# Where the last rounds read layer 1 out of PSUM, and the precision of four late units, in a three-layer interaction network

## The chip, the core and the metric

One core of a Trainium2 chip runs the whole program. The metric is the device time of one execution in microseconds, lower is better. The core has a matrix engine (TensorE, PE in the rows; its weight loads are PEld), a vector engine (VectorE, DVE), a scalar engine (ScalarE, ACT), a general engine (GpSimd, POOL) and a queue that issues transfers (SyncE, SP). Each engine executes its own instructions in the order in which they are written and meets the others by semaphores.

## The reference

1024 rows of 39 looked-up fields, each a vector of 16 numbers, pass through three layers of pairwise products. Layer i multiplies each field of the input with each field of the layer's state and contracts the products with a weight matrix of 128 columns; half of the outputs of the first two layers becomes the next state, the rest goes straight to the sum. Three dense layers follow.

```python
for i, (W, b) in enumerate(zip(Ws, bs)):
    Wr = W.reshape(F0, Fk, L)
    z = jnp.einsum('bfd,bgd->bfgd', x, h)
    cur = jax.nn.relu(jnp.einsum('bfgd,fgl->bld', z, Wr) + b[None, :, None])
    if i != n - 1:
        h = cur[:, :L // 2]
        direct = cur[:, L // 2:]
    else:
        direct = cur
    outs.append(direct)
...
h = jnp.maximum(h @ W_top1 + b_top1, 0.0)
h = jnp.maximum(h @ W_top2 + b_top2, 0.0)
y = h @ W_top3
```

## The kernel before

The 1024 x 16 columns are cut into 32 steps of 512 columns. A software pipeline runs over rounds r = -3 to 31. In round r, units 0 to 9 contract layer 1 of step r + 1, units 10 to 19 layer 2 of step r, and units 20 to 23 layer 0 of step r + 3. The last rounds are shorter: rounds 29 and 30 have units 0 to 19 alone, and round 31 has units 10 to 19. (r, u) below is unit u of round r. A unit is up to 256 rows of products by 512 columns, and its kind says how it is made:

- F, full precision: VectorE makes the product in SBUF (L618), TensorE contracts it with two full matrix products, which the trace shows as four instructions (L987). ScalarE and GpSimd have no part in it.
- G: VectorE makes the product, ScalarE copies it rounded to `zh` (`hi`, L816), GpSimd subtracts to get the rest `zl` (L359), and TensorE makes six faster instructions: two each of `zh` with the weights' low part (L1004), `zh` with the high part (L1005), and `zl` with the high part (L1012).
- P: the same split with the product held in PSUM (`curY`), in two halves of 512 columns; VectorE makes product and rest of each half (L684, L696), ScalarE rounds each (L801). In round 29 the parts of a P unit follow it at a distance of two and four units, in round 30 at one and two: the first rest and the second product stand before the product of the unit behind it, the second rest before that of the unit two behind.
- D: like G, with the rest made by VectorE (L705).

Rounds 29 and 30 both have the kinds `GPGGFGPGGF FGPGGFGPGG` for units 0 to 19. Units 3, 8, 14 and 19 are F in the early rounds; from round 25 or 26 on `kind` makes them G, with weights of their own (`wh_late`, `wl_late`).

The rings: products lie in a ring of 7 slots, `zh` and `zl` in rings of 4. The semaphore `z_ready` counts products made, `z_used` counts units that TensorE has finished.

When a layer's sum is complete, ScalarE reads it out of PSUM with bias and relu. `take0` and `take1` do this for layers 0 and 1 in seven instructions each (all L850): number 6, called `DIRECT`, writes the part that goes to the sum, numbers 0 to 5 write copies of the next state to the PSUM tile `h1` or `h2`. `take1(r, i)` reads layer 1 of step r + 1. `take2(s)` reads layer 2 of step s in one instruction, at unit 1 of round s + 1 (`LAST_AT`), after a wait until TensorE has finished unit (s, 19). Which unit each read of layer 1 follows on ScalarE is written out in `round_` of ScalarE: up to round 28, `DIRECT` after unit 18, 0 to 3 after unit 20, 4 and 5 after unit 21; in rounds 29 and 30 all seven in a row at the round's end.

Who waits for the reads of `take1(29, ...)`: VectorE's `sum_direct(30)`, a short reduction (L709) which stands behind the product of (30, 3), and VectorE and TensorE before unit (30, 10). Who waits for `take1(30, ...)`: `sum_direct(31)`, and TensorE before the dense layers (L1104, L1110, L1118, L1126), which stand between rounds 30 and 31. After round 31 a short end of the dense layers for the last 128 rows follows (L1156 to L1174).

Of the kernel before, what the change touches and what calls it, by code (L numbers as in the profile page):

```python
# [14 lines left out]
B, F, D, L = 1024, 39, 16, 128  # L15
# [5 lines left out]
STEPS = B * D // N  # L21
# [15 lines left out]
UNITS = len(KINDS)  # L37
A_END, C_END = 10, 20
# [6 lines left out]

LATE_A, LATE_C = (3, 8), (14, 19)
LATE = LATE_C + LATE_A
LATE_FROM = 25

POOL_FROM = 11  # L50
# [2 lines left out]
def present(r, u):  # L53
    if u < A_END:
        return -1 <= r <= STEPS - 2
    if u < C_END:
        return 0 <= r <= STEPS - 1
    return -3 <= r <= STEPS - 4


def kind(r, u):
    if ((r >= LATE_FROM and u in LATE_C) or (r > LATE_FROM and u in LATE_A)):
        return "G"

    k = KINDS[u]
    if k == "P":
        return "P" if r in IN_PSUM else "D"
    return "D" if k == "G" and (r < 0 or (r == 0 and u < POOL_FROM)) else k


def fresh(r):

    return (r + 3) % PER_B == 0
# [72 lines left out]
def cin_tower(nc, dense, ids, tables, w_top1, b_top1, w_top2, b_top2, w_top3, w0, w1, w2, b0, b1, b2, out):  # L146
# [4 lines left out]
    with ExitStack() as ctx:  # L151
        def sb(name, shape, dt=F32):
            return ctx.enter_context(nc.sbuf_tensor(name, shape, dt))
# [36 lines left out]
        wl = sb("wl", [P, UNITS - nf, 2, L], F32R)  # L190
        wh_late = sb("wh_late", [P, len(LATE), 2, L], F32R)
        wl_late = sb("wl_late", [P, len(LATE), 2, L], F32R)

        def full_at(u):
            return KINDS[:u].count("F")
# [116 lines left out]
        def bank(r, layer):  # L312

            if r < 0:
                return curY if layer == 0 and r != -2 else curM[r == -2]

            return xk[:, :] if (r, layer) == (STEPS - 3, 2) else curM[(r + (layer - 1) % 3) % 2]
# [25 lines left out]
        def _(pool):  # L343
# [9 lines left out]
            def subtract(r, u):  # L353
                n = split_rows(u)
                before = ring_before(r, u, NL)
                if before is not None:
                    pool.wait_ge(z_used, NUM[before] + 1)
                pool.wait_ge(hi_ready, SNUM[r, u] + 1)
                nc.gpsimd.tensor_tensor(zl[0:n, SNUM[r, u] % NL, :], z[0:n, z_slot(r, u), :],  # L359
                                        zh[0:n, SNUM[r, u] % NH, :], ALU.subtract).then_inc(lo_pool, 1)  # L360

            def weight_lo_late(n):
                pool.wait_ge(w_hi, HI_OPS + n + 1)
                nc.gpsimd.tensor_tensor(wl_late[:, n, :, :], wf[:, full_at(LATE[n]), :, :], wh_late[:, n, :, :],
                                        ALU.subtract).then_inc(w_lo, 1)

            def round_(r):
# [16 lines left out]
                for n, u in enumerate(spread):  # L384
                    if kind(r, u) == "G":
                        subtract(r, u)
                    if r == LATE_FROM and 2 <= u < 2 + len(LATE):
                        weight_lo_late(u - 2)
# [388 lines left out]
        def _(act):  # L777
# [26 lines left out]
            def hi(r, u):  # L804
                second = behind(r, u, 1)
                if second:
                    hi_half(*second, 1)
                if kind(r, u) == "P":
                    hi_half(r, u, 0)
                elif kind(r, u) != "F":  # L810
                    n = split_rows(u)
                    act.wait_ge(z_ready, NUM[r, u] + 1)
                    before = ring_before(r, u, NH)
                    if before is not None:
                        act.wait_ge(z_used, NUM[before] + 1)
                    nc.scalar.activation(zh[0:n, SNUM[r, u] % NH, :], z[0:n, z_slot(r, u), :],  # L816
                                         ACT.Copy).then_inc(hi_ready, 1)
# [11 lines left out]
            def copy_emb(b):  # L829
                act.wait_ge(gathered[b % 2], 16 * F * (b // 2 + 1) - 16 * FIRST_FIELDS * (b % 2 == 0))  # L830
                nc.scalar.activation(emb[b % 2][:, F * D:].rearrange("p (k c) -> p k c", k=K - 1),
                                     emb[b % 2][:, 0:F * D].unsqueeze(1).to_broadcast([P, K - 1, F * D]),
                                     ACT.Copy).then_inc(emb_copied, 1)
# [8 lines left out]
            def copy_xc(t):  # L842
                act.wait_ge(turned, t + 1)
                if t >= 3:
                    act.wait_ge(xT_written[t % 2], 32 * (t // 2))
                nc.scalar.activation(xc[t % 2][:, :].rearrange("p (b d) -> p b d", d=DQ),
                                     xk_bank(t)[0:F, :].rearrange("p (d b) -> p b d", d=DQ), ACT.Copy).then_inc(xc_copied, 1)
# [4 lines left out]
            DIRECT = 6  # L852
            DIRECT_FIRST = (DIRECT, 0, 1, 2, 3, 4, 5)

            def take(i, h, cur, bias, done, to):

                if i < 2:
                    relu(h[i * H:(i + 1) * H, 0:N], cur[0:H, :], bias[0:H, :], done)
                elif i < 6:
                    p, f = (i - 2) * Q, (i - 1) % 2 * Q  # L860
                    relu(h[p:p + Q, N:2 * N], cur[f:f + Q, :], bias[f:f + Q, :], done)
                else:
                    relu(to, cur[H:P, :], bias[H:P, :], done)

            def take0(r, i):
                s = r + 2
                if i == DIRECT:
                    act.wait_ge(z_used, NUM[r - 1, UNITS - 1] + 1)
                    if s >= 2:
                        act.wait_ge(sumA, s - 1)  # L870
                if i == 0 and r >= -1:
                    act.wait_ge(z_ready, NUM[r, A_END - 1] + 1)
                take(i, h1, l0_bank(s), bias0, read0, direct[s % 2][0:H, :])

            def take1(r, i):
                s = r + 1
                if i == DIRECT:
                    act.wait_ge(z_used, NUM[r, A_END - 1] + 1)
                    if s >= 2:
                        act.wait_ge(sumA, s - 1)  # L880
                if i == 0:
                    act.wait_ge(z_ready, NUM[r, C_END - 1 if r >= 0 else UNITS - 1] + 1)
                take(i, h2, bank(r, 1), bias1, read1, direct[s % 2][H:P, :])

            def weight_hi_late(n):
                nc.scalar.activation(wh_late[:, n, :, :], wf[:, full_at(LATE[n]), :, :], ACT.Copy).then_inc(w_hi, 1)

            def take2(s):
                act.wait_ge(z_used, NUM[s, C_END - 1] + 1)
                if s >= 1:  # L890
                    act.wait_ge(sumB, s)
                relu(last[:, :], bank(s, 2), bias2[:, :], read2)

            def round_(r):
                for u in range(UNITS):
                    if present(r, u):
                        hi(r, u)
                    if r == -2 and u == UNITS - 1:
                        for i in DIRECT_FIRST:
                            take0(r, i)  # L900
                    if r == LATE_FROM and 2 <= u < 2 + len(LATE):
                        weight_hi_late(u - 2)
                    if u == SPREAD_AT and r >= 1 and fresh(r) and r <= STEPS - 4:
                        copy_emb((r + 3) // PER_B)
                    if u == LAST_AT and r >= 1:
                        take2(r - 1)
                    if u == COPY_AT and 0 <= r <= STEPS - 4:
                        copy_xc(r + 3)
                    if u == A_END - 1 and r == -1:
                        for i in DIRECT_FIRST:  # L910
                            take0(r, i)

                    if 0 <= r <= STEPS - 3:
                        for i in {8: [DIRECT], A_END: [0, 1, 2], A_END + 1: [3, 4], A_END + 2: [5]}.get(u, []):
                            take0(r, i)
                    if 0 <= r <= STEPS - 4:
                        for i in {C_END - 2: [DIRECT], C_END: [0, 1, 2, 3], C_END + 1: [4, 5]}.get(u, []):
                            take1(r, i)
                    if u == UNITS - 1 and (r == -1 or STEPS - 4 < r <= STEPS - 2):
                        for i in DIRECT_FIRST:  # L920
                            take1(r, i)

# [5 lines left out]
            for r in range(FIRST, 1):  # L928
                round_(r)
            for r in range(1, LAST):  # L930
                round_(r)
# [39 lines left out]
        def _(pe):  # L971
# [8 lines left out]
            def contract(r, u, cur, start, stop):  # L980
# [9 lines left out]
                else:  # L990
                    h, l, w = SNUM[r, u] % NH, SNUM[r, u] % NL, split_at(u)
                    w_low, w_high = wl, wh
                    if KINDS[u] == "F":
                        w, w_low, w_high = LATE.index(u), wl_late, wh_late
                        if r <= LATE_FROM + 1:
                            pe.wait_ge(w_hi, HI_OPS + w + 1)
# [204 lines left out]
```

## Time and profile before

| | us |
|---|---|
| runs | 1285.22, 1287.26, 1286.15 (median 1286.15) |
| the profiled execution's own time | 1286.31 |
| its span in the trace | 1284.2 |
| busy: PE / DVE / POOL / ACT | 1215.5 / 1113.8 / 1036.5 / 816.4 |

The span runs from the first to the last instruction; 2.1 us of the profiled execution lie around it. Busy time of PE counts overlapping instructions once. A start in the timeline is us from the span's start, followed by the duration; a figure in square brackets is the idle time of the engine before the instruction, and behind the arrow stands what ended it.

### The profile page before, as it was taken

The page shows a single profiled execution, that of the slowest core. Times are in us where ns is not written, and L with a number is a line of the kernel's source. Part 1 is how long each engine was busy: PE and PEld are TensorE (multiplying, and loading weights), DVE is VectorE, ACT ScalarE, POOL GpSimd, SP SyncE. Part 2 cuts the span into 40 slices and gives each one's busy share as a digit, 9 for nine tenths or more (in the row PEclk, how much of TensorE's full clock was granted, in tenths as well). Part 3 has the DMA queues.
Part 4 walks back from the last instruction along what each step waited for, and adds up shares of the span by engine and source line. Part 5 has one row for each costly group of instructions (what it writes and reads, how often), then busy time and mean ns, then how long its engine had stood idle before and what let it go on. Part 6 is the DMA issues. An engine that isn't in the chain of part 4 may idle for free.

```text
span 1284.2 us, 14380 instructions
## 1 busy us (share of the span) xinstructions
PE 1215.5 (95%) x4180; PEld 767.5 (60%) x4180; DVE 1113.8 (87%) x1274; ACT 816.4 (64%) x1115; POOL 1036.5 (81%) x629
## 2 busy tenths in 40 slices
PE   0598999999999999999999999999999999999899
PEld 0254566666666666666666666666666666766545
DVE  2189999999999999999999999999999999999753
ACT  1147566666676667666676667666666778777553
POOL 7458888888988888888988888888988778888733
PEclk9999999999999999999999999999999999999999
DMA  8193466655555566655555666655455665654100
GB/s 185 24 230 93 108 143 147 146 134 116 111 125 119 132 146 147 146 130 115 112 123 122 135 146 147 147 123 118 113 117 123 139 144 144 142 119 118 33 1 1
DMA packets 102510, 156.17 MB, mean 122 GB/s; under 512 B 20811, under 2 KB 32988, under 8 KB 102322
## 3 DMA queue, kind: packets, MB, share of 16 engines
q1 hardware_dynamic: 92256, 152.56, 50.2%
q0 software_dynamic: 10176, 2.70, 2.1%
q8 instruction: 33, 0.54, 0.2%
q14 instruction: 45, 0.37, 0.1%
HBM read 151.31 MB, written 6.19 MB: 123 GB/s over the span
## 4 chain that ended last, share of the span: by engine, by line
PE 80%; DVE 7%; issue 4%; POOL 4%; ACT 4%; DMA 0%; another core or an unknown queue 0%; DVEq 0%; ACTq 0%; POOLq 0%
PE curM L987 36%; PE curM L1004 13%; PE curM L1012 13%; PE curM L1005 13%; DVE z L618 4%; POOL emb L348 3%; ACT h L850 2%; PE xk L976 2%; DVE zl L705 1%; ACT zh L816 1%; DVE zl L696 1%; POOL zl L359 1%; DVE curY L684 1%; DVE z L669 0%; PE h L1110 0%
## 5 line engine op out<-in xcount | busy, mean ns | idle before, releaser
L359 POOL TENSOR_TENSOR zl<-z,zh 128x1024 fp32r<-128x1024 f32 (+1 forms) x301 | 718.4, 2396 | 146.9 <-ACT zh L816 131.0
L618 DVE TENSOR_TENSOR z<-xr,h 128x1024 f32<-128x1024 f32 x456 | 548.4, 1212 | 3.8 <-issue 3.1
L987 PE MATMUL curM<-z,wf 128*128 128x512 f32 (+3 forms) x1220 | 537.4, 600 | 1.0 <-ACT h L850 0.9
L816 ACT ACTIVATE zh<-z 128x1024 fp32r<-128x1024 f32 (+1 forms) x320 | 337.8, 1056 | 291.1 <-DVE z L618 150.6
L348 POOL DMA_INDIRECT emb<-in_tbl_dram,idx x312 | 311.5, 998 | 89.7 <-issue 54.5
L1004 PE MATMUL curM<-zh,wl 128*128 128x512 f32 (+1 forms) x816 | 374.9, 459 | 4.8 <-issue 3.2
L987 PEld LDWEIGHTS curM<-z,wf 128*128 128x128 f32 (+3 forms) x1220 | 214.7, 188 | 237.6 <-issue 217.2
L1005 PE MATMUL curM<-zh,wh 128*128 128x512 f32 (+1 forms) x816 | 321.4, 394 | 0.0
L1012 PE MATMUL curM<-zl,wh 128*128 128x512 f32 (+1 forms) x816 | 255.5, 394 | 9.6 <-POOL zl L359 5.1
L850 ACT ACTIVATE h<-curM,bias 64x512 f32<-64x512 f32 x372 | 240.4, 646 | 20.0 <-DVE z L618 9.9
L696 DVE TENSOR_TENSOR zl<-curY,zh 128x512 fp32r<-128x512 f32 x240 | 164.9, 687 | 71.0 <-ACT zh L801 69.1
L1004 PEld LDWEIGHTS curM<-zh,wl 128*128 128x128 f32 (+1 forms) x816 | 154.7, 190 | 63.9 <-issue 35.4
L1005 PEld LDWEIGHTS curM<-zh,wh 128*128 128x128 f32 (+1 forms) x816 | 154.3, 189 | 57.5 <-issue 29.9
L1012 PEld LDWEIGHTS curM<-zl,wh 128*128 128x128 f32 (+1 forms) x816 | 153.0, 189 | 49.7 <-POOL zl L359 7.5
L801 ACT ACTIVATE zh<-curY 128x512 fp32r<-128x512 f32 x240 | 141.6, 590 | 45.6 <-PE curM L1012 33.0
L684 DVE TENSOR_TENSOR curY<-xr,h 128x512 f32<-128x512 f32 x240 | 166.0, 692 | 4.1
L669 DVE TENSOR_TENSOR z<-xk,xs 117x1024 f32<-117x1024 f32 x116 | 120.6, 1080 | 1.2 <-PE curM L987 1.2
L618 DVE TENSOR_TENSOR z<-xq,h 128x1024 f32<-128x1024 f32 x64 | 77.4, 1211 | 0.0
L850 ACT ACTIVATE direct<-curM,bias 64x512 f32<-64x512 f32 x62 | 42.4, 684 | 1.6
L850 ACT ACTIVATE last<-curM,bias 128x512 f32<-128x512 f32 x31 | 21.2, 684 | 31.2 <-PE curM L987 21.0
L976 PEld LDWEIGHTS xk<-ident,emb 128*117 128x117 f32 x120 | 28.5, 285 | 13.7 <-issue 11.1
L705 DVE TENSOR_TENSOR zl<-z,zh 128x1024 fp32r<-128x1024 f32 (+1 forms) x19 | 28.6, 1507 | 5.6 <-ACT zh L816 3.8
(140 smaller groups left out, 391.0 us busy)
## 6 DMA issues: line engine op xcount, KB each, us to landing
xr<-xT SPq DMA_DIRECT2D x384, 192.0 KB
xs<-xT SPq DMA_DIRECT2D x279, 156.0 KB
xq<-xT SPq DMA_DIRECT2D x64, 256.0 KB
emb<-in_tbl_dram,idx POOLq DMA_INDIRECT x312
xs<-xT SPq DMA_DIRECT2D x62, 78.0 KB
xT<-xc SPq DMA_DIRECT2D x31, 78.0 KB
xr<-in_L_rec_W_dram SPq DMA_DIRECT2D x16, 144.0 KB
xT<-xc SPq DMA_DIRECT2D x31, 40.0 KB
```

The costliest lines, as they stand in the source:

```text
L348: nc.gpsimd.indirect_dma_start(out=emb[slot][:, f * D:(f + 1) * D], out_offset=None, in_=tables[f], in_offset=bass.IndirectOffsetOnAxis(ap ...
L359: nc.gpsimd.tensor_tensor(zl[0:n, SNUM[r, u] % NL, :], z[0:n, z_slot(r, u), :], zh[0:n, SNUM[r, u] % NH, :], ALU.subtract).then_inc(lo_poo ...
L618: return nc.vector.tensor_tensor(z[:, slot, :].rearrange("p (a n) -> p a n", a=2), x, h, ALU.mult)
L684: nc.vector.tensor_tensor(curY[:, :], xr[s % 2][:, q * N:(q + 1) * N], h[:, a * N:(a + 1) * N], ALU.mult).then_inc(done, 1)
L696: nc.vector.tensor_tensor(zl[:, SNUM[r, u] % NL, cols], curY[:, :], zh[:, SNUM[r, u] % NH, cols], ALU.subtract).then_inc(lo_dve if a == 1 ...
L801: nc.scalar.activation(zh[:, SNUM[r, u] % NH, a * N:(a + 1) * N], curY[:, :], ACT.Copy).then_inc(hi_ready if a == 0 else hi_second, 1)
L816: nc.scalar.activation(zh[0:n, SNUM[r, u] % NH, :], z[0:n, z_slot(r, u), :], ACT.Copy).then_inc(hi_ready, 1)
L850: nc.scalar.activation(dst, src, ACT.Relu, bias=bias).then_inc(done, 1)
L987: mm = nc.tensor.matmul(cur[:, :], wf[rows, full_at(u), a, :], z[rows, z_slot(r, u), a * N:(a + 1) * N], start=start and i == 0, stop=stop ...
L1004: nc.tensor.matmul(cur[:, :], w_low[rows, w, a, :], zh[rows, h, cols], start=start and a == 0, stop=False)
L1005: nc.tensor.matmul(cur[:, :], w_high[rows, w, a, :], zh[rows, h, cols], start=False, stop=False)
L1012: mm = nc.tensor.matmul(cur[:, :], w_high[rows, w, a, :], zl[rows, l, a * N:(a + 1) * N], start=False, stop=stop and a == n - 1)
```

## The change

In rounds 29 and 30, units 8 and 19 are F again, as in the early rounds: four units in all. In round 29 the read `DIRECT` of layer 1 stands after unit 18, and the six others are moved behind units 0, 1 and 2 of round 30, two at each (for unit 1, behind `take2(29)`, which stands there too). The reads of round 30 stay in a row at its end. The round numbers in the code: `STEPS` is 32, `C_END` 20, `UNITS` 24.

```diff
+SHORT, LONGER = (STEPS - 3, STEPS - 2), (8, 19)
...
 def kind(r, u):
+    if r in SHORT and u in LONGER:
+        return "F"
     if ((r >= LATE_FROM and u in LATE_C) or (r > LATE_FROM and u in LATE_A)):
         return "G"
...
                     if 0 <= r <= STEPS - 4:
                         for i in {C_END - 2: [DIRECT], C_END: [0, 1, 2, 3], C_END + 1: [4, 5]}.get(u, []):
                             take1(r, i)
-                    if u == UNITS - 1 and (r == -1 or STEPS - 4 < r <= STEPS - 2):
+                    if r == STEPS - 3 and u == C_END - 2:
+                        take1(r, DIRECT)
+                    if r == STEPS - 2 and u < 3:
+                        for i in range(2 * u, 2 * u + 2):
+                            take1(r - 1, i)
+                    if u == UNITS - 1 and r in (-1, STEPS - 2):
                         for i in DIRECT_FIRST:
                             take1(r, i)
```

## Rows read from the trace of the kernel before

**Rows 1.** Busy time by stretch: PE, PEld, DVE, ACT, POOL, then granted clock.

```profile
1165.00:1194.40 29.40, 29.34 (x115) 20.64 (x113) 25.06 (x29) 21.76 (x30) 24.68 (x11) 1.00 0.36 99
...
1203.00:1233.50 30.50, 26.28 (x96) 16.58 (x94) 21.25 (x25) 17.43 (x23) 23.20 (x10) 1.00 0.00 1
1233.50:1261.00 27.50, 27.46 (x83) 12.87 (x84) 14.00 (x14) 11.70 (x18) 6.57 (x3) 1.00 0.00 1
```

**Rows 2.** Timeline of ScalarE from (29, 17) to `take2(29)`.

```profile
1187.74 0.60 ACT L801 ACTIVATE zh<-curY 128x512 fp32r<-128x512 f32 x1 [0.31 <-DVE curY L684]
...
1190.66 4.00 ACT L850 ACTIVATE h<-curM,bias 64x512 f32<-64x512 f32 x6
1194.69 1.06 ACT L816 ACTIVATE zh<-z 128x1024 fp32r<-128x1024 f32 x1
1195.65 0.58 ACT L801 ACTIVATE zh<-curY 128x512 fp32r<-128x512 f32 x1
1196.13 0.68 ACT L850 ACTIVATE last<-xk,bias 128x512 f32<-128x512 f32 x1
```

**Rows 3.** Timeline of VectorE from products (29, 19), (30, 0) to `sum_direct(30)`.

```profile
1187.61 2.35 DVE L618 TENSOR_TENSOR z<-xr,h 128x1024 f32<-128x1024 f32 x2
...
1190.59 0.70 DVE L684 TENSOR_TENSOR curY<-xr,h 128x512 f32<-128x512 f32 x1
1196.33 0.69 DVE L696 TENSOR_TENSOR zl<-curY,zh 128x512 fp32r<-128x512 f32 x1 [5.04 <-ACT zh L801]
...
1200.52 0.68 DVE L709 TENSOR_REDUCE zq<-direct 128x128 f32<-128x512 f32 x1
```

**Rows 4.** Timeline of TensorE: (29, 19), first and sixth instruction of (30, 0).

```profile
1192.80 0.39 PE L1004 MATMUL xk<-zh,wl_late 128*128 128x512 f32 x1
...
1193.72 0.62 PE L1012 MATMUL xk<-zl,wh_late 128*128 128x512 f32 x2
1195.89 0.47 PE L1004 MATMUL curM<-zh,wl 128*128 128x512 f32 x1 [1.55 <-ACT zh L816]
...
1198.32 1.22 PE L1012 MATMUL curM<-zl,wh 128*128 128x512 f32 x2 [1.26 <-POOL zl L359]
```

**Rows 5.** Chain that ended last: unit (29, 15), of kind F, on TensorE.

```profile
1187.13 1.73 PE xk L987 x4
```

**Rows 6.** Timeline of GpSimd: last three rests of round 29, two of 30.

```profile
1185.84 7.12 POOL L359 TENSOR_TENSOR zl<-z,zh 128x1024 fp32r<-128x1024 f32 x3 [0.18 <-PE xk L1012]
...
1227.07 4.75 POOL L359 TENSOR_TENSOR zl<-z,zh 128x1024 fp32r<-128x1024 f32 x2 [1.70 <-ACT zh L816]
```

**Rows 7.** Timeline of ScalarE: round 31's `take2`, waiting on TensorE.

```profile
1275.81 0.69 ACT L850 ACTIVATE last<-curM,bias 128x512 f32<-128x512 f32 x1 [6.10 <-PE curM L1012]
```

**Rows 8.** Timeline of TensorE: what that `take2` waited for.

```profile
1275.15 0.63 PE L1012 MATMUL curM<-zl,wh_late 128*128 128x512 f32 x2
```

**Rows 9.** Timeline of ScalarE at the end of round 30.

```profile
1225.87 1.06 ACT L816 ACTIVATE zh<-z 128x1024 fp32r<-128x1024 f32 x1 [0.53 <-DVE z L618]
1227.60 1.06 ACT L816 ACTIVATE zh<-z 128x1024 fp32r<-128x1024 f32 x1 [0.67 <-DVE z L618]
1228.69 0.68 ACT L850 ACTIVATE direct<-curM,bias 64x512 f32<-64x512 f32 x1
1229.39 4.00 ACT L850 ACTIVATE h<-curM,bias 64x512 f32<-64x512 f32 x6
```

**Rows 10.** Timeline of VectorE there: product (30, 19), `sum_direct(31)`.

```profile
1226.35 1.21 DVE L618 TENSOR_TENSOR z<-xr,h 128x1024 f32<-128x1024 f32 x1
1233.50 0.69 DVE L709 TENSOR_REDUCE zq<-direct 128x128 f32<-128x512 f32 x1 [5.94 <-ACT h L850]
```

**Rows 11.** Timeline of TensorE there: ends of (30, 18), (30, 19), first dense product.

```profile
1229.53 0.73 PE L1012 MATMUL curM<-zl,wh 128*128 128x512 f32 x2 [0.31 <-POOL zl L359]
...
1231.87 0.74 PE L1012 MATMUL curM<-zl,wh_late 128*128 128x512 f32 x2 [0.69 <-POOL zl L359]
1233.54 0.70 PE L1104 MATMUL h<-dT,xs 16*128 16x512 f32 x2 [0.93 <-ACT h L850]
```

**Rows 12.** Busy time by stretch, as rows 1: the round's start, in steps of 2 us.

```profile
1198.00:1200.00 2.00, 1.69 (x4) 1.40 (x5) 2.00 (x3) 1.44 (x2) 0.26 (x1) 0.53 0.00 0
1200.00:1202.00 2.00, 2.00 (x7) 1.52 (x7) 2.00 (x3) 1.06 (x1) 1.89 (x1) 0.62 0.00 0
```

## The prediction

> **What bounds the kernel now.** I read the busy time by stretch first, then the timelines of the engines where one stretch meets the next. Round 29 belongs to TensorE: it works 29.34 of 29.40 us, without a gap [rows 1]. VectorE is ahead there: product (29, 19) is ready at 1188.82 (1187.61 and 1.21 of the two products' 2.35 us) [rows 3], and TensorE ends that unit at 1193.72 + 0.62 = 1194.34 [rows 4]. Then the lead is lost. ScalarE does the seven reads in a row, the last six from 1190.66 for 4.00 us, and only behind them the rounding of (30, 0) at 1194.69 and of the first half of (30, 1) at 1195.65 [rows 2]. TensorE stands for 1.55 us and 1.26 us [rows 4], VectorE for 5.04 us [rows 3]. From there to 1227.6 VectorE sets the pace, and TensorE has 30.50 - 26.28 = 4.22 us of idle time [rows 1]. At the round's end seven reads stand again behind the last rounding, and the dense layers start at 1233.54, when they are done [rows 9, 11]. After that TensorE works 27.46 of 27.50 us [rows 1]: what starts it earlier ends the kernel earlier, one for one.
>
> **Part 1, the four units as F.** An F unit holds TensorE 1.73 us [rows 5]. In a G unit four instructions take 1193.72 - 1192.80 = 0.92 us, 0.23 each, so six take 1.38 [rows 4]. Each unit costs TensorE 0.35 us more. It takes from ScalarE one rounding of 1.06 us [rows 9] and from GpSimd one rest of 7.12 / 3 = 2.37 us [rows 6]. In round 29 TensorE has no gap to hide it, so two units move its end from 1194.34 to 1195.04. By itself that is no loss, since (30, 0) starts at 1195.89 [rows 4]. In round 30 it disappears in the idle 4.22 us. The slot of an F product is freed by TensorE and no longer by GpSimd; the seven products until its next use take at least 7 x 1.14 = 8.0 us of VectorE (2.35 - 1.21 = 1.14 from one to the next), and TensorE's lag was 1194.34 - 1188.82 = 5.5 us, now 6.2, so no wait: cost nothing, cover 1.8 us. No transfer is added or moved.
>
> **Part 2, the reads of round 29.** `DIRECT` after unit 18 moves the rounding of the second half of (29, 17) from 1187.74 [rows 2] to some 1188.15; its rest is made behind the product (30, 0), which ends at 1189.96 [rows 3]. Cost nothing, cover 1.2 us. The rounding of (29, 19) is gone, so that of (30, 0) runs when its product is there, 1190.0 to 1191.05. Reads 0 and 1 follow (2 x 0.67, from 4.00 / 6), then the first half of (30, 1), 1192.4 to 1193.0. The 5.04 us wait of VectorE shrinks by 3.3 us.
>
> But next on ScalarE stands `take2(29)`, and it waits for TensorE to end round 29, at 1195.04. In the kernel before it ran at 1196.13, when that had long happened. A read of the same kind starts 0.03 us after TensorE's end (1275.15 + 0.63 against 1275.81) [rows 7, 8]. So ScalarE stands for 2.0 us, and behind it are queued reads 2 and 3, the second half of (30, 1), the rounding of (30, 2), reads 4 and 5. From 1195.07: 0.70 for `take2` (the spacing 1228.69 to 1229.39 [rows 9]), 2 x 0.67, 0.48 to 0.60 for the half [rows 2], 1.08 for the rounding, 2 x 0.67. The sum is 4.94 to 5.06, the end 1200.01 to 1200.13. VectorE's `sum_direct(30)` needs all seven reads; a reduction starts 0.11 us after its last read (1229.39 + 4.00 against 1233.50) [rows 9, 10]: 1200.12 to 1200.24, where it ran at 1200.52 [rows 3]. VectorE reaches this point earlier: its rest of (30, 1) can start at some 1197.8 and the product (30, 3) ends at 1199.6. The old wait of 5.04 us becomes two, for the half and for the reads, and VectorE gains 0.28 to 0.40 us; I take **0.35**. All products of the round stand behind, so they come this much earlier. TensorE and GpSimd, fed by them, are not late: (30, 0) is ready for TensorE when it comes at 1195.04.
>
> **Part 3, the end of round 30.** The rounding of (30, 19), 1227.60, is gone. `DIRECT` follows that of (30, 18): 1225.87 + 1.09 = 1226.96. Read 0 needs product (30, 19), ready at 1226.35 + 1.21 = 1227.56 [rows 10], and ScalarE is there at 1227.66. Six reads end at 1231.66, and TensorE follows 0.15 later (1233.39 against 1233.54 [rows 9, 11]), at 1231.81 in place of 1233.54: 1.73. TensorE itself: the rest of (30, 18) by GpSimd ends at 1229.45 (half of 4.75 [rows 6]) and lets it go at 1229.53; it ends at 1230.26 at the latest [rows 11], and F takes it to 1231.99: 1.55 by this bound. The wait of 0.69 us for the rest of (30, 19) is gone as well. I take **1.6**; what is late next is TensorE's F unit and the reads at once, within 0.2 us.
>
> **Sum.** 0.35 + 1.6 = 1.95 us off 1286.31 of the profiled execution, 1284.36. The median of the runs is 0.16 lower, which gives 1284.2.
>
> **The clock.** After the gaps of 1.55 and 1.26 us the granted clock falls to 0.53 and 0.62 for 4 us, the 1.2 GHz level for most of it [rows 12]. It costs nothing now, as TensorE then waits for others anyway. The Trainium skill (TensorE: Matmul & The Clock Gate, "HAM oscillation") says that a TensorE left idle is gated to half its clock until it has been busy again. It speaks against this change in one respect: TensorE comes to (30, 0) sooner, and then waits in pieces for a later supply. By that page such a gap could put the F unit at the end at half clock; the rival for it below has its price from the rows.
>
> **Rivals.** *B, the longer round 29 costs nothing.* If TensorE took the two F units without ending later, `take2(29)` would end its wait 0.70 us sooner, VectorE would gain 1.05 in place of 0.35, and the time would be 1283.5. Against it stands the missing gap, 0.06 us in 29.40 [rows 1]. For it: ends of matrix products are modelled, and the lag could be smaller than it looks.
>
> *C, the first gain is not there and the second is cut.* If the chain behind `take2(29)` runs 0.4 us longer than my sum, the 0.35 is gone; if the F unit at the end meets a falling clock, its 1.73 us doubles. Then the 1.6 becomes -0.1: 1284.55 for the first alone, 1286.3 for both. The point from which it decides is `take2(29)` ending its wait after 1195.5.
>
> *D, slower: the clock falls on the path.* The dense layers are 27.5 us of TensorE with nothing to hide a slower clock [rows 1]. Stretches of 4 us at half clock, as the one seen [rows 12], cost 2 us each there: one takes the gain back, and 10 us at the lower level would cost 5 and give 1289.2. It decides from 4 us on, and from 9 us the kernel is slower by more than 0.2%. Against it: TensorE is busy before them with F at 1230 to 1232, where it had idled 0.93 us at full clock [rows 11].
>
> *E, the reads are no longer in anyone's way.* All that the reads cost in front would come back: 3.3 us at the first, 1.6 at the second, 1281.3. It needs `take2(29)` not to wait, which needs TensorE 2 us earlier at the end of round 29. No row allows it.
>
> **How the numbers follow.** My case (A) 0.58, with its own range 1283.5 to 1285.0; B 0.17, C 0.17, D 0.06, E 0.02. Its own runs spread over 2 us, so the range for 8 in 10 is 1282.6 to 1286.3: it holds A, B and C. What a measurement of this kernel can tell from no change is about 0.2%, 2.6 us; A is 1.95, so it counts as no difference unless it is undersized by a third, B (2.65) is just over. Faster 0.27 (B, E and the edge of A), same 0.67, slower 0.06.
>
> **What would show it.** After: `take2(29)` preceded by an idle 2 us of ScalarE, ended by TensorE at about 1195.05; two waits of VectorE between 1194 and 1200.2 in place of the 5.04; `sum_direct(30)` ended by a read, near 1200.2; products from there 0.35 us earlier; no L816 after 1226.6 in round 30; first L1104 at 1231.6 to 1231.7, with at most 0.2 us idle before it. I am wrong if `take2(29)` doesn't wait, if the granted clock falls between 1225 and 1260, or if `sum_direct(30)` is more than 0.5 us off.

## The result: 0.3% faster, and two steps of the forecast found again

The changed kernel takes 1282.85 us (median, 1282.15 to 1283.9), the kernel before on the same chip 1286.49. The ratio is 0.9969, 95% interval 0.9958 to 0.998: a gain of some 4.0 us by the ratio and 3.6 by the medians. The forecast was 1284.2, no difference most likely, from a gain of 1.95 us. The profiled execution took 1283.14 us, its span 1281.4: some 1.8 us lie around the span, where 2.1 did in the kernel before.

To see where the time went I followed one kind of instruction, VectorE's short reductions, which stand at fixed places of each round. This is the kernel before (start, duration; the one in round 29 and the last one, in round 31):

```profile
1177.68 0.68 DVE L709 TENSOR_REDUCE zq<-last 128x128 f32<-128x512 f32 x1
...
1276.53 0.69 DVE L709 TENSOR_REDUCE zq<-last 128x128 f32<-128x512 f32 x1 [7.29 <-ACT last L850]
```

and this the kernel after, in rounds 29 and 30, between the rounds 30 and 31, and in round 31:

```profile
1177.01 0.68 DVE L713 TENSOR_REDUCE zq<-last 128x128 f32<-128x512 f32 x1
...
1199.31 0.69 DVE L713 TENSOR_REDUCE zq<-direct 128x128 f32<-128x512 f32 x1 [0.47 <-ACT h L854]
...
1230.57 0.69 DVE L713 TENSOR_REDUCE zq<-direct 128x128 f32<-128x512 f32 x1 [4.21 <-ACT h L854]
...
1273.67 0.69 DVE L713 TENSOR_REDUCE zq<-last 128x128 f32<-128x512 f32 x1 [7.28 <-ACT last L854]
```

They come 0.67, 1.21, 2.93 and 2.86 us earlier than in the kernel before (the middle ones against [rows 3, 10]). The first 0.67 is there from the first reduction on, at 109.00 before and 108.34 after, and stays within 0.06 up to round 29: it arises in the set-up, which the change doesn't touch. The changed rounds bring 1.21 - 0.67 = 0.54 at their start (**front** below), and 2.86 - 1.21 = 1.65 at their end (**end**), 2.19 us together. With the set-up's 0.67 and the 0.3 us that lie no longer around the span, this is the 3.17 us between the two profiled executions (1286.31 and 1283.14).

The front, on ScalarE of the kernel after: the reads of layer 1 are L854, `take2(29)` the one from `xk`.

```profile
1190.40 1.33 ACT L854 ACTIVATE h<-curM,bias 64x512 f32<-64x512 f32 x2
1191.66 0.58 ACT L805 ACTIVATE zh<-curY 128x512 fp32r<-128x512 f32 x1
1194.39 0.69 ACT L854 ACTIVATE last<-xk,bias 128x512 f32<-128x512 f32 x1 [2.15 <-PE xk L996]
1195.10 1.31 ACT L854 ACTIVATE h<-curM,bias 32x512 f32<-32x512 f32 x2
1196.35 0.57 ACT L805 ACTIVATE zh<-curY 128x512 fp32r<-128x512 f32 x1
1196.83 1.04 ACT L820 ACTIVATE zh<-z 128x1024 fp32r<-128x1024 f32 x1
1197.89 1.32 ACT L854 ACTIVATE h<-curM,bias 32x512 f32<-32x512 f32 x2
```

ScalarE stands for 2.15 us before `take2(29)`, until TensorE has ended round 29, and everything else is queued behind it. VectorE's wait of 5.04 us [rows 3] has become three, of 1.74, 2.14 and 0.47 us, the third one that of the reduction at 1199.31. These are the first two:

```profile
1192.34 0.69 DVE L700 TENSOR_TENSOR zl<-curY,zh 128x512 fp32r<-128x512 f32 x1 [1.74 <-ACT zh L805]
...
1197.03 0.69 DVE L700 TENSOR_TENSOR zl<-curY,zh 128x512 fp32r<-128x512 f32 x1 [2.14 <-ACT zh L805]
```

The end, on TensorE: the rest of (30, 18), unit (30, 19) in full precision, the first dense product with no idle time before it, where 0.93 us stood [rows 11].

```profile
1228.33 0.72 PE L1021 MATMUL curM<-zl,wh 128*128 128x512 f32 x2 [0.34 <-POOL zl L363]
1228.89 1.88 PE L996 MATMUL curM<-z,wf 128*128 128x512 f32 x4
1230.70 0.70 PE L1113 MATMUL h<-dT,xs 16*128 16x512 f32 x2
```

By stretch (columns as in rows 1), TensorE has no gap in round 29 and none in the dense layers:

```profile
1165.00:1193.50 28.50, 28.50 (x108) 19.57 (x107) 25.49 (x31) 18.74 (x25) 21.61 (x10) 1.00 0.37 100
...
1203.00:1231.00 28.00, 25.48 (x90) 15.29 (x93) 20.61 (x24) 14.72 (x21) 16.60 (x7) 1.00 0.00 1
1231.00:1258.50 27.50, 27.50 (x83) 12.69 (x77) 13.93 (x14) 11.92 (x18) 6.93 (x3) 1.00 0.00 1
```

### The profile page after: what moved, and what is told of

It reads as the page before. It is cut to its first block, busy times and chain, and to the rows that moved or that the text cites. A ratio compares the mean times of both kernels' runs of the same rounds, so it can differ in the third digit from the quotient of the medians.

```text
span 1281.4 us, 14348 instructions
## 1 busy us (share of the span) xinstructions
PE 1217.5 (95%) x4172; PEld 766.3 (60%) x4172; DVE 1113.7 (87%) x1274; ACT 811.8 (63%) x1111; POOL 1026.7 (80%) x625
## 4 chain that ended last, share of the span: by engine, by line
PE 84%; DVE 6%; issue 4%; POOL 3%; ACT 3%; DMA 0%; DVEq 0%; ACTq 0%; POOLq 0%
PE curM L996 37%; PE curM L1013 13%; PE curM L1021 13%; PE curM L1014 13%; DVE z L622 3%; POOL emb L352 3%; PE xk L985 2%; ACT h L854 1%; DVE zl L709 1%; ACT zh L820 1%; PE h L1071 1%; DVE zl L700 1%; DVE z L673 1%; PE h L1119 0%; PE h L1127 0%
## 5 line engine op out<-in xcount | busy, mean ns | idle before, releaser
L363 POOL TENSOR_TENSOR zl<-z,zh 128x1024 fp32r<-128x1024 f32 (+1 forms) x297 | 708.8, 2396 | 154.4 <-ACT zh L820 137.6
L820 ACT ACTIVATE zh<-z 128x1024 fp32r<-128x1024 f32 (+1 forms) x316 | 333.5, 1056 | 291.7 <-DVE z L622 155.2
L854 ACT ACTIVATE h<-curM,bias 64x512 f32<-64x512 f32 x372 | 240.4, 646 | 20.7 <-DVE z L622 10.8
L854 ACT ACTIVATE direct<-curM,bias 64x512 f32<-64x512 f32 x62 | 42.4, 683 | 1.6
L854 ACT ACTIVATE last<-curM,bias 128x512 f32<-128x512 f32 x31 | 21.2, 684 | 31.6 <-PE curM L996 25.5
```

The source lines that it names most:

```text
L854: nc.scalar.activation(dst, src, ACT.Relu, bias=bias).then_inc(done, 1)
```

## The experiments

For each kernel the table has the distances between its trace and the first one of the kernel before, read from the same reductions: set-up (up to round 29), front, end, and front and end together; negative is earlier. Then the difference of the medians and the ratio with its interval, against the kernel before on the same chip.

| kernel | set-up | front | end | both | medians | ratio (95%) |
|---|---|---|---|---|---|---|
| changed | -0.67 | -0.54 | -1.65 | -2.19 | -3.64 | 0.9969 (0.9958 to 0.998) |
| changed, again | -5.42 | -0.53 | -1.66 | -2.19 | -2.37 | 0.9977 (0.9967 to 0.9987) |
| units only | -6.29 | -1.59 | -1.63 | -3.22 | -3.37 | 0.9969 (0.9957 to 0.9981) |
| reads only | -6.15 | -1.20 | +1.71 | +0.51 | -0.86 | 0.9993 (0.9984 to 1.0002) |
| take2 late | -5.87 | -2.42 | -1.62 | -4.04 | -4.56 | 0.9961 (0.9947 to 0.9974) |
| before, again | -0.73 | 0.00 | +1.70 | +1.70 | +0.63 | 1.0001 (0.9992 to 1.001) |
| reads early | -1.25 | -3.21 | -1.62 | -4.83 | -6.44 | 0.9951 (0.9937 to 0.9964) |
| unit 19 only | +0.53 | -0.86 | -1.63 | -2.49 | -3.41 | 0.997 (0.9958 to 0.9982) |
| last unit only | -0.49 | 0.00 | -1.62 | -1.62 | -2.52 | 0.9979 (0.997 to 0.9988) |
| gap | +0.31 | -0.54 | -0.55 | -1.09 | -2.63 | 0.9977 (0.9967 to 0.9987) |

The four from "changed, again" to "take2 late" ran together on another chip, where the kernel before takes 1280.68 us; their set-up of -5 to -6 most likely goes with that chip, of which there is no trace of the kernel before.

The intervals reach 1.2 to 1.7 us to either side, so the times alone don't put these kernels in order among themselves. What follows on single steps rests on the traces, where front and end repeat within some 0.01 us.

**The changed kernel again.** No edit.

> The changed kernel once more, beside the others. Its timeline against the one before shows three steps: products 0.65 us earlier from the set-up on to the end of round 29, 1.21 earlier from the L713 reduction of round 30 on, 2.93 earlier from the dense layers on. Theory A (the set-up's 0.65 us and what lies outside the span are chance, other in each execution): the step of round 30 is 0.5 us and that of the end 1.7 us again, together 2.2 to 2.3 us, while the set-up's part changes in size or sign; the time is 2.3 us below the kernel before, within 0.7 us. Theory B (the changed program is also faster where nothing was changed, by its layout): the set-up's 0.65 us comes again, and the time is 3.5 to 4 us below.

Front and end repeat within 0.01 us. The distance of the set-up does not say anything across two chips; the time, 2.4 us lower by the medians and 2.9 by the ratio (1.7 to 4.2 by its interval), lies nearer to theory A and doesn't exclude B.

**Units only.**

```diff
+SHORT, LONGER = (STEPS - 3, STEPS - 2), (8, 19)
...
 def kind(r, u):
+    if r in SHORT and u in LONGER:
+        return "F"
```

> Only the four units as F; the reads of round 29 stay in a row at its end. Theory A (it is ScalarE's freed rounding of (29, 19), 1.06 us, and the place of take2(29), that count): the seven reads start 1.6 us earlier than before, since the first of them no longer waits for product (29, 19) to be rounded; the rest of the first half of (30, 1) comes at 1194.7 in place of 1196.33, take2(29) waits only 0.4 us and delays nobody; the reduction of round 30 is 1.6 us earlier, the dense layers 3.3 us earlier, the time 3.3 us below the kernel before: better than the change as made. Rival (the spread of the reads is what gains in front, the units gain at the end only): 1.7 us below the kernel before.

The front is 1.59, three times that of the whole change, and the time is 3.4 us below the kernel before. The seven reads still stand in a row, but what stood in front of them, the rounding of (29, 19), is gone; when ScalarE comes to `take2(29)`, TensorE is nearly done (0.43 us of waiting):

```profile
1182.77 4.00 ACT L854 ACTIVATE h<-curM,bias 64x512 f32<-64x512 f32 x6
1186.80 1.06 ACT L820 ACTIVATE zh<-z 128x1024 fp32r<-128x1024 f32 x1
...
1188.77 0.69 ACT L854 ACTIVATE last<-xk,bias 128x512 f32<-128x512 f32 x1 [0.43 <-PE xk L991]
```

**Reads only.** The change without the two lines in `kind`.

> Only the reads of round 29 spread over the first units of round 30; no unit changes its kind. Theory A: TensorE ends round 29 0.7 us sooner than with the units, so take2(29) starts at 1194.4 on the scale of the kernel before and the chain behind it ends 0.7 us sooner: reduction of round 30 1.2 us earlier, nothing at the round's end, 1.2 us below the kernel before. Rival (the reads in a row cost what VectorE stood for, 5.04 us, and spreading them brings most of that): 3 us or more below. The parts then add up, by theory A, to 3.3 + 1.2 = 4.5 us, and the whole is only 2.3.

The front is 1.20: TensorE ends round 29 some 0.7 us sooner without the F units, `take2(29)` waits 1.13 us instead of 2.15, and the difference to the changed kernel, 1.20 - 0.53 = 0.67, is what two F units cost TensorE (2 x 0.35 in the forecast). So the parts don't add up: 1.20 and 1.59 in front give 0.54. Where (29, 19) is F, spreading the reads takes 1.05 us away. The +1.71 at the end is not the edit's: this execution's dense layers met a fall of the granted clock to half (by stretch, columns as in rows 1), and the kernel before shows one too, below:

```profile
1227.00:1229.00 2.00, 2.00 (x7) 0.95 (x4) 2.00 (x3) 0.00 (x0) 0.00 (x0) 0.71 0.04 8
1229.00:1231.00 2.00, 2.00 (x3) 0.67 (x2) 2.00 (x3) 0.41 (x1) 0.00 (x0) 0.50 0.00 0
```

**take2 late.** In the changed kernel:

```diff
-                    if u == LAST_AT and r >= 1:
+                    if u == (3 if r == STEPS - 2 else LAST_AT) and r >= 1:
                         take2(r - 1)
```

> The changed kernel, with take2(29) moved from unit 1 to unit 3 of round 30, behind all reads of layer 1. It takes away what stands in front of ScalarE's queue while TensorE ends round 29. Theory A (the wait of take2(29) is what limits the gain of the spread): VectorE's two waits of 1.74 and 2.14 us become one of 1.7 and one under 0.5; the reduction of round 30 is 1.8 us earlier than in the changed kernel, the time 4.1 us below the kernel before. Rival (ScalarE's work alone, seven reads and four roundings, is what limits): the same time as the changed kernel, within 0.4 us.

The one wait taken out of the queue brings 1.89 us in front. ScalarE reads on where it had stood (its second pair of reads, timeline):

```profile
1187.08 1.31 ACT L854 ACTIVATE h<-curM,bias 32x512 f32<-32x512 f32 x2
```

VectorE's second wait of 2.14 us is gone; the reduction waits 0.81 us for the last read, more than I had put:

```profile
1187.15 0.69 DVE L700 TENSOR_TENSOR zl<-curY,zh 128x512 fp32r<-128x512 f32 x1 [1.73 <-ACT zh L805]
...
1192.23 0.69 DVE L713 TENSOR_REDUCE zq<-direct 128x128 f32<-128x512 f32 x1 [0.81 <-ACT h L854]
```

**The kernel before, again.** No edit.

> The kernel before, unchanged, timed against itself and with a new profile. Theory A (part of the measured difference is chance of the set-up and of where the granted clock falls for 3.4 us): its timeline runs parallel to the first profile of the kernel before from round 1 to round 30, at a constant distance that differs from it by up to 1 us on one chip; the ratio is 1.000 within 0.0005. If its clock falls within the dense layers, as it did in the run with the reads alone (3.4 us at the lower level, 1.7 us lost), the kernel before has that loss in some executions, and the changed kernel, whose TensorE comes to the dense layers without a gap, has it less often: this would be the missing 0.7 us. Rival (the clock falls there only by chance of one execution): no fall between round 30 and the end.

The ratio is 1.0001, and the front is 0.00. But the dense layers of this trace hold what the first profile of the same kernel didn't show. The granted clock falls at the start of the dense layers (by stretch, columns as in rows 1):

```profile
1233.00:1235.00 2.00, 2.00 (x10) 0.73 (x9) 1.97 (x3) 0.38 (x1) 0.00 (x0) 0.85 0.03 8
1235.00:1237.00 2.00, 2.00 (x4) 0.70 (x3) 2.00 (x3) 0.00 (x0) 0.00 (x0) 0.50 0.00 0
1237.00:1239.00 2.00, 2.00 (x5) 0.88 (x4) 2.00 (x3) 0.69 (x1) 0.00 (x0) 0.79 0.00 0
```

On TensorE's timeline this is just behind the gap of 0.94 us, and eight dense instructions take 5.40 us, where they take 3.70 at full clock:

```profile
1232.81 0.70 PE L1104 MATMUL h<-dT,xs 16*128 16x512 f32 x2 [0.94 <-ACT h L850]
...
1233.88 5.40 PE L1110 MATMUL h<-zs,xs 128*128 128x512 f32 x8
```

All from there on is 1.70 us later, to the end. So the kernel before pays this in some of its executions; how often, its three traces can't tell.

**Reads early.** take2 late, and each pair of reads one unit earlier:

```diff
-                    if r == STEPS - 2 and u < 3:
-                        for i in range(2 * u, 2 * u + 2):
+                    if r == STEPS - 3 and u == C_END - 1:
+                        for i in (0, 1):
+                            take1(r, i)
+                    if r == STEPS - 2 and u < 2:
+                        for i in range(2 * u + 2, 2 * u + 4):
                             take1(r - 1, i)
```

> The run with take2 late, and each pair of reads one unit earlier: 0 and 1 at the end of round 29, 2 and 3 behind unit 0 of round 30, 4 and 5 behind the first half of unit 1. Theory A (ScalarE's queue is what the products of (30, 1) to (30, 3) wait for; with take2 late only the reads stand before them): the reduction of round 30 no longer waits for a read; it comes 3.0 us earlier than in the kernel before (the run with take2 late: 2.4), the dense layers 4.7 us earlier, the time 4.7 us below. Rival (TensorE or GpSimd sets round 30 by then, TensorE having 28 us of work from 1195.0 on): the gain stays at the 4.1 us of the run with take2 late.

Front 3.21, both 4.83 us, 1280.21 us against 1286.65: the lowest ratio of these kernels, 0.9951 (0.9937 to 0.9964). The reduction no longer waits at all. Of the 5.04 us, one wait of VectorE is left before it:

```profile
1191.86 0.69 DVE L700 TENSOR_TENSOR zl<-curY,zh 128x512 fp32r<-128x512 f32 x1 [1.83 <-ACT zh L805]
```

Behind the reduction a wait of 1.07 us has appeared, at 1200.67, for the rounding of the next P unit; it takes nothing from the distances above, since 3.21 is still there when the dense layers start.

**Unit 19 only.**

```diff
-SHORT, LONGER = (STEPS - 3, STEPS - 2), (8, 19)
+SHORT, LONGER = (STEPS - 3, STEPS - 2), (19,)
```

> The changed kernel with unit 19 alone as F in rounds 29 and 30; unit 8 stays as before. Theory A (take2(29) waits for TensorE, which has no gap in round 29, so each F unit there delays all of round 30 by 0.35 us): reduction of round 30 0.85 us earlier than in the kernel before (changed kernel: 0.5), dense layers 2.6 us earlier, 0.35 us below the changed kernel. Rival (TensorE absorbs unit 8): the same as the changed kernel.

The front grows from 0.54 to 0.86: the F unit (29, 8) costs 0.32 us of the path, one for one through `take2(29)`. The total against the changed kernel (0.997 and 0.9969) is too small a difference to be seen in the times.

**Last unit only.** In the kernel before:

```diff
 def kind(r, u):
+    if (r, u) == (STEPS - 2, C_END - 1):
+        return "F"
```

> The kernel before with one unit changed, (30, 19) as F; everything else as before. Theory A (the gain of the end is this unit alone): the reductions of round 30 keep the distance of the set-up, the dense layers come 1.73 us earlier against them; TensorE goes from unit 19 into the dense layers with less than 0.2 us of idle time, and the granted clock doesn't fall in the dense layers. Time 1.7 us below the kernel before, and up to 0.9 more where that one has the fall of the clock in half of its executions. Rival (the end gains only together with the earlier start of round 30): under 1 us.

Front 0.00, end 1.62. One unit gives three quarters of what the trace shows for the whole change (1.62 of 2.19), and the times show 2.5 to 2.7 us: 0.9 to 1.1 more than the trace.

**The kernel before once more**, a third trace of it, and **the gap** put back: the changed kernel with three short instructions on ScalarE among the reads of round 30, so that TensorE stands again before the dense layers; two further traces of it follow.

> A second look at the kernel before, for where its granted clock falls and for its set-up. Theory A: the set-up differs from the other look by some tenths of a us; the clock falls once in or just behind the gaps of 1.55 and 1.26 us at the start of round 30 or of 0.93 us before the dense layers, and costs 1.7 us only where it reaches into the dense layers. Rival: no difference between two looks on one chip.

```diff
+        spare = sb("spare", [P, 768])
...
                         for i in DIRECT_FIRST:
+                            if r == STEPS - 2 and i in (3, 4, 5):
+                                nc.scalar.activation(spare[:, 256 * (i - 3):256 * (i - 2)], bt1[:, 0:1].to_broadcast([P, 256]), ACT.Relu)
                             take1(r, i)
```

> The changed kernel with three added instructions on ScalarE among the reads of round 30 (256 columns each into a spare tile, some 0.4 us each), so that the last reads come 1.2 us later and TensorE stands about 1.2 us before the dense layers, as it stood 0.94 us there in the kernel before. Theory C (a gap of TensorE there is what lets the granted clock fall within the dense layers): time 1.2 us above the changed kernel (1.1 us below the kernel before by medians) and a fall of 3.4 us just behind the gap in some executions, each costing 1.7 us. Rival (the gap has nothing to do with it, falls come by chance anywhere): 1.2 us above the changed kernel, and no fall there in three looks.

> The same kernel, a second look at its granted clock. Theory C: in two of three looks or so a fall at the start of the dense layers; rival: none.

> The same kernel, a third look at its granted clock. Theory C: with the other two looks, at least one fall at the start of the dense layers; rival: none in all three.

The third trace of the kernel before has its set-up 0.48 us earlier than the first one, a front and an end of -0.01 and 0.01, and no fall in the dense layers. The three traces of the kernel with the gap have set-ups of +0.31, -0.18 and -1.06, the same program on one chip. TensorE stands 1.00 to 1.02 us before the dense layers, and none of the three has the fall behind it; the eight instructions take 3.70 us each time. This is the first of them:

```profile
1232.77 0.70 PE L1116 MATMUL h<-dT,xs 16*128 16x512 f32 x2 [1.02 <-ACT h L855]
...
1233.84 3.70 PE L1122 MATMUL h<-zs,xs 128*128 128x512 f32 x8
```

So theory C, that this gap alone lets the clock fall, is not borne out, though three traces can't exclude a rare fall. The time is 2.6 us below the kernel before, where theory C had put 1.1.

## Why the forecast was wrong, point by point

- **What bounds the kernel**: right. VectorE paces round 30, TensorE the rest, and what starts the dense layers earlier ends the kernel earlier: in every trace of a changed kernel the lead at the start of the dense layers is still there in the last reduction to within 0.11 us, apart from the one with the fall.
- **Part 1**, 0.35 us per F unit on TensorE: right, 0.32 by unit 8, and 0.67 by the two of round 29 together.
- **Part 2**, `take2(29)` as the new wait: right in place and size, 2.15 us where 2.0 stood. The gain was 0.54 instead of 0.35: the chain behind the wait took 4.92 us to the reduction (1194.39 to 1199.31) and not 5.05 to 5.17. Of the 0.13 us to the lower bound 0.09 come from a rounding that starts before the read ahead of it has ended (it stands 1.25 us behind the start of two reads and not 1.34). The reduction itself ran 0.9 us before the 1200.2 of the forecast, more than the 0.5 that I had named as a sign of being wrong; 0.67 of this is the set-up. What I didn't do was price the parts singly. With the units alone the front is three times as large, so the words "part 2 gains 0.35" hide that the spread of the reads costs 1.05 us where the units are F.
- **Part 3**, 1.6 us: right, 1.65, with TensorE's F unit last.
- **The sum and the time**: this is the step that failed. The trace moved by 2.19, 0.24 more than my 1.95 and from the parts that I had named; the time moved by 3.6 to 4.0. I took 1.95 straight off the time of one profiled execution, and so put two terms at nothing without a reason: the time around the span, and the clock of the dense layers in the other executions of the kernel before.
- **The first term, around the span**: 0.3 us. In the 78 executions with (30, 19) as G whose span is on record (kernel before and reads only) 2.00 to 2.13 us of the time lie outside the span, in the 61 with it as F 1.68 to 1.81. This comes with that one unit (last unit only has 1.68 to 1.78). Why is open.
- **The second term, the clock, and rival D**: the price is real, 1.70 us for one fall of 3.4 us, but on the wrong side. I priced it as something that the change could bring; the kernel before has it in some executions, and my one profile of it, whose dense layers ran at full clock, didn't show it. Of four traces of kernels with (30, 19) as G two have the fall at the dense layers' start (one of three of the kernel before, and reads only); of ten with it as F none.
- **How much the second term has to carry**: the eight rows of the table with (30, 19) as F are 0.7 to 1.9 us faster by the ratio than their front and end (ratio times the time of before: 4.0 against 2.19, 2.9 against 2.19, 4.0 against 3.22, 5.0 against 4.04, 6.3 against 4.83, 3.9 against 2.49, 2.7 against 1.62, 3.0 against 1.09), while reads only, with G there, isn't (0.9 against 1.20). Six of the eight differences are smaller than what their intervals reach to one side. Less the 0.3 us around the span, 0.4 to 1.6 are left, 0.95 in the mean: a fall in about every second execution of the kernel before would make it up. The set-up's 0.67 us is chance, by the spread of 1.37 us between three traces of one program, and should mostly cancel in medians.
- **What speaks for the falls beside the traces**: the mean granted clock of every timed execution. On the two chips of the table's last five rows 14 of 46 executions of the kernel before have 0.992, as the profiled one with the fall has, and all of these take 1287.1 to 1288.0 us; the ten at 0.995 or 0.996 take 1286.2 in the mean. Of the eleven of last unit only none has 0.992, and their mean time is 1284.1 at 0.993 and 1284.5 at 0.995. Within each kernel and chip, 0.001 less of the clock goes with 0.45 us more time (standard error 0.07) over 77 executions of kernels with (30, 19) as G, and with 0.06 us (0.08) over 59 of kernels with it as F. The mean clock doesn't tell where a fall lay, so that the falls explain the whole of the missing time is argued from this and the counts, not shown.
- **Which idle time lets the clock fall** is open. The Trainium skill (TensorE: Matmul & The Clock Gate, "HAM oscillation") warns of idle gaps between matrix products; the traces agree in direction. Both falls began 1.6 us into the dense layers, behind idle times of TensorE of 0.69 us before the rest of (30, 19) and 0.93 or 0.94 before the dense layers. But the other two traces with G have the same idle times and no fall, and in the kernel with the gap the second alone was put back.
- **Rivals B, C, E**: none of them. B's price, 1.05 in front if the two units cost TensorE nothing, is what reads only measured as 1.20. E, the reads in nobody's way, I called impossible with `take2` in place, and it was; moving `take2` and the pairs of reads makes it real, 3.21 of the 3.3 us in front.

## What to carry to other kernels

Before a wait is spread over an engine's queue, look at what else stands in that queue with a wait of its own: here one read that needed TensorE's end blocked everything behind it, and moving it by two units was worth more than moving six reads. Price each part of a change alone and with the other, since two that shorten the same wait don't add up. And where a stretch is bound by TensorE and begins behind idle time, one profile doesn't tell its clock: take two or three profiles before a forecast within some tenths of a per cent, and set the mean clock of the timed executions against their times.

## What was not expected of the hardware

Two traces of one program on one chip differ by up to 1.4 us in the set-up, and then run parallel within some 0.15 us for over 1000 us.

One fall of the granted clock to its lower level, 1.2 GHz, lasts 3.4 us and costs 1.70 us in full where TensorE is the bound. At the start of round 30 it costs nothing, although every trace of the kernel before, and that of last unit only, has one there, of 3.4 us in two of them and of 6.8 in the other two: the front is the same within 0.01 us. None of the ten other traces has a fall there; TensorE's longest single idle time at that place is 1.22 us in them, where those four have one of 1.5 and one of 1.26 or so.

With one late unit in full precision instead of split, 0.3 us less of the time lies outside the span from the first to the last instruction, in every execution.
